# Cross attention: scores by row in six units, and the two halves of dense at other places in TensorE's order

## What is computed

```
cq  = heads(rms_norm(hidden) @ cq_w)                      # 112 tokens, 16 heads
ck, cv = split(encoder_outputs @ ckv_w)                   # 375 rows
p   = softmax(cq * scale @ ck.T)                          # per head, not causal
hidden = hidden + (p @ cv) @ cdense_w                     # "context", then "dense"
```

## Time and profile before

| | us |
|---|---|
| median of 3 runs (2385.53 to 2386.26) | 2385.78 |
| the profiled execution | 2383.2 |
| its span | 2381.4 |
| TensorE busy, share of the span | 2174.7, 91% |
| VectorE busy | 1342.4, 56% |
| ScalarE busy | 1073.9, 45% |
| cross attention, from the first scores to the last copy | 1082 to 1663 |

### The profile page before, as it was taken

The page is one execution under the profiler, slowest core; times in us unless marked ns, Lnnn a source line. Parts: engine busy times, 40 slices in busy tenths (PEclk is TensorE's granted clock), DMA queues, the critical chain, the costliest instruction groups (busy, mean ns, idle before and its releaser), DMA issues.

```text
span 2381.4 us, 46501 instructions
## 1 busy us (share of the span) xinstructions
PE 2174.7 (91%) x19368; PEld 1820.1 (76%) x19368; DVE 1342.4 (56%) x1887; ACT 1073.9 (45%) x1842; POOL 841.8 (35%) x706
## 2 busy tenths in 40 slices
PE   5899996999879988988999999997899999999998
PEld 4899985887756667876777777775788888888887
DVE  4655545877669994435666666663444434435332
ACT  4334434333157774533555555554434434334432
POOL 1101017677513213540222111110555555555553
PEclk8999998999979998997999999999899999999999
DMA  6334335565454445632111111110643443443331
GB/s 201 133 115 141 123 88 180 202 234 208 146 169 130 138 121 215 253 149 74 49 41 41 49 39 49 41 33 29 222 146 124 137 131 120 148 133 109 111 116 45
DMA packets 107057, 293.56 MB, mean 123 GB/s; under 512 B 14424, under 2 KB 18360, under 8 KB 100216
## 3 DMA queue, kind: packets, MB, share of 16 engines
q1 hardware_dynamic: 86624, 229.63, 29.9%
q0 software_dynamic: 18720, 60.29, 6.9%
q10 hardware_dynamic: 1504, 0.68, 0.1%
HBM read 221.36 MB, written 69.18 MB: 122 GB/s over the span
## 4 chain that ended last, share of the span: by engine, by line
PE 73%; DVE 17%; ACT 4%; DMA 3%; issue 2%; POOL 1%; SPq 0%; POOLq 0%; DVEq 0%; ACTq 0%
PE ps L109 19%; PE ps L111 18%; PE ps L110 18%; PE ps L1554 4%; PE ps L1573 3%; PE ps L1591 3%; DVE f_arena L1166 3%; DVE c_max L1161 3%; DVE f_arena L962 3%; ACT f_arena L1474 3%; DVE c_sum L1172 2%; DMA f_arena<-mem_t 1%; PE ps L607 1%; DVE f_arena L958 1%; PE ps L1576 1%
## 5 line engine op out<-in xcount | busy, mean ns | idle before, releaser
L109 PE MATMUL ps<-r_arena 128*128 128x512 f32 (+6 forms) x2410 | 905.6, 376 | 39.1 <-DVE r_arena L177 18.2
L177 POOL TENSOR_TENSOR r_arena<-f_arena,r_arena 128x512 fp32r<-128x512 f32 (+1 forms) x438 | 586.5, 1364 | 868.7 <-ACT r_arena L1455 438.4
L111 PE MATMUL ps<-r_arena 128*128 128x512 f32 (+6 forms) x2410 | 883.8, 367 | 0.0
L110 PE MATMUL ps<-r_arena 128*128 128x512 f32 (+6 forms) x2410 | 883.6, 367 | 0.0
L109 PEld LDWEIGHTS ps<-r_arena 128*128 128x128 f32 (+2 forms) x2410 | 456.0, 189 | 131.8 <-issue 37.6
L111 PEld LDWEIGHTS ps<-r_arena 128*128 128x128 f32 (+2 forms) x2410 | 455.9, 189 | 66.1
L110 PEld LDWEIGHTS ps<-r_arena 128*128 128x128 f32 (+2 forms) x2410 | 457.0, 190 | 60.1
L199 ACT CAST r_arena<-f_arena 128x512 fp32r<-128x512 f32 x400 | 235.5, 620 | 171.3 <-PE ps L111 131.7
L1675 DVE TENSOR_REDUCE e_negmax<-ps 112x3 f32<-112x1125 f32 (+1 forms) x160 | 225.2, 1408 | 106.7 <-PE ps L1554 103.8
L1474 ACT ACTIVATE f_arena<-ps 125x1792 f32<-125x1792 f32 x96 | 159.9, 1666 | 97.9 <-PE ps L1576 97.4
L1959 DVE SCALAR_TENSOR_TENSOR f_arena<-f_arena,ps 128x512 f32<-128x512 f32 (+1 forms) x88 | 57.4, 652 | 234.8 <-ACT f_arena L1850 234.8
(11 more groups left out here) (197 smaller groups left out, 2714.9 us busy)
## 6 DMA issues: line engine op xcount, KB each, us to landing
f_arena<-weights SPq DMA_DIRECT2D x400, 256.0 KB, 3.0
f_arena<-rows SPq DMA_DIRECT2D x14, 1160.0 KB, 5.2
f_arena<-qk_rows SPq DMA_DIRECT2D x32, 448.0 KB, 3.9
f_arena<-mem_e SPq DMA_DIRECT2D x32, 376.0 KB, 3.1
f_arena<-mem_t SPq DMA_DIRECT2D x16, 750.0 KB, 9.8
f_arena<-mem_n SPq DMA_DIRECT2D x8, 1500.0 KB
h_rows<-f_arena SPq DMA_DIRECT2D x7, 1160.0 KB, 4.8
f_arena<-h_rows SPq DMA_DIRECT2D x7, 1160.0 KB, 5.2
```

The costliest lines, as they stand in the source:

```text
L109: first = pe.matmul(out, w_hi, x_hi, start=start, stop=False)
L110: pe.matmul(out, w_hi, x_lo, start=False, stop=False)
L111: return first, pe.matmul(out, w_lo, x_hi, start=False, stop=stop)
L177: return engine.tensor_tensor(out, source, high.bitcast(F32), ALU.subtract)
```

## The change

Scores by row go from five units to six: four of three heads and two of two heads, so that none is in bank 3 any more. Two waits go with that: the last unit's wait for the copy out of bank 3, and context's wait for all maxima. In TensorE's order dense half 0 moves behind scores 3, and dense half 1 behind scores 4, ahead of the new scores 5. The orders of ScalarE, VectorE, GpSimd and SyncE are not changed, but for VectorE's sixth maximum, which its loop over the units brings.

```diff
-S_UNITS, KEY_UNITS = 5, 3
+S_UNITS, KEY_UNITS = 6, 3
@@
-        s_heads = [range(3 * u, 3 * u + 3 if u < S_UNITS - 1 else HEADS) for u in range(S_UNITS)]
+        s_heads = [range(3 * u, 3 * u + 3) for u in range(4)] + [range(12, 14), range(14, 16)]
@@ scores(b, u)
-                if u == S_UNITS - 1 and b >= 2:
-                    pe.wait_ge(e_cd_out, b - 1)
@@ context(b, t)
-                if t == 0:
-                    pe.wait_ge(e_maxed, S_UNITS * min(b + 2, BATCHES))
@@ TensorE's loop
                     scores(s, 2)
                 if 1 <= s <= BATCHES:
                     scores_by_key(s - 1, 0)
-                if s >= 2:
-                    dense(s - 2, 0)
                 if s < BATCHES:
                     scores(s, 3)
                 if s >= 2:
-                    dense(s - 2, 1)
+                    dense(s - 2, 0)
                 if 1 <= s <= BATCHES:
                     scores_by_key(s - 1, 1)
                 if s < BATCHES:
                     scores(s, 4)
+                if s >= 2:
+                    dense(s - 2, 1)
+                if s < BATCHES:
+                    scores(s, 5)
                 if 1 <= s <= BATCHES:
                     scores_by_key(s - 1, 2)
                 if s + 1 < BATCHES:
```

## The result

The changed kernel takes 2480.07 us (median of 4 runs, 2475.86 to 2481.95) against 2386.02 us (4 runs) before: a ratio of 1.0391, 95% interval 1.0373 to 1.0409. It is slower by 94 us. I had forecast 48.7 us more, and a range that ended at 2462 us. The profiled execution took 2481.95 us, its span 2480.1 us.

What follows compares the result with a forecast made beforehand. TensorE, busy 91% of the span, was taken to set the pace, with one hole before key unit 2. Terms 45.3 + 1.6 + 0.4 + 1.4 = 48.7 us on 2385.8 gave 2434.5 us; range 2425 to 2462.

Steps and rivals of the forecast that it cites:

- The chain through ScalarE's queue: Full steps: dense's copy waits for dense half 1, exponentials queue behind it, key unit 2 waits; 1.51 us more a step.
- 30 full steps x 1.51: Cross attention, steps 2 to 31, with both dense and scores: 1.51 us more each, 45.3 us in all.
- Two units for one: Four-head scores unit split into two and two: nothing in full steps, 1.6 us more in the first, 0.4 in the second.
- The 0.4 us for the second step: Second step of the stage, which has no dense: key unit 2 loads 0.4 us later, 0.8 at the lower clock.
- Waits taken out: Scores 4's wait for the copy of dense's result and context's wait for all maxima: removing them changes nothing.
- The end: Step after the last scores: exponential 1 starts at 1652.47 instead of 1651.10, 1.4 us more.
- The clock falls too: Rival: TensorE's clock falls in full steps, up to 2.9 us each; one step in three adds 29 us, 2464 us; chance 0.17.
- The first rival: Full steps: the copy does not delay exponential 1; 0.39 us more a step, 2399.5 us in all; chance 0.09.
- The faster rival: Full steps: exponentials alone set the pace, 0.34 us less a step, some 2377 us in all; chance 0.02.
- the reduction's bound: The two-head maximum takes at least 0.89 us; the faster rival needed under 0.45 us.
- the step's bounds: Extra time of a full step taken as 1.35 to 1.80 us, given as 2428 to 2446 us for the kernel.
- The wait of 1.25 us: Before the change, TensorE's matmuls wait 1.25 us ahead of key unit 2 for exponential 1, 28 times in full steps.

Runs made afterwards that it cites:

- the run with only the small units: The changed kernel with six units kept but both halves of dense back behind key unit 0 and scores 3; 2408.84 us, ratio 1.0084.

## Why the prediction was right in its mechanism and wrong in its sum

- **The chain through ScalarE's queue: right.** Forecast were loads at 2.20, 2.89, 3.77, 4.64, 5.33, 6.47 and 8.53; the trace has 2.21, 2.92, 3.81, 4.68, 5.39, 6.49 and 8.58. The term "30 full steps x 1.51" measures 1.53 in the run with two useless matmuls. The swap of two ScalarE instructions shows the cause. The runs with two and with five useless matmuls behave as the kernel that I forecast, at full clock in all full steps, and took 2433.9 and 2433.7 us for 2434.5. From the first scores to the last copy of the stage the trace with two is 49.3 us longer than before, for 48.7. That is 42.8 in the 28 steps (forecast 42.3), 1.3 ahead of them (2.0), 1.6 in the two steps behind them (3.0) and 3.5 in the end (1.4). That the three small terms make up for each other is luck.
- **The Trainium skill's rule** from "PSUM — Partial Sum Buffer", section "Engine vs sequencer instructions", that ScalarE's queue is strict first in, first out: the trace agrees. Exponential 1 stood ready for 1.9 us (key unit 1 done by about 1361.3, start at 1363.18) behind a copy that waited.
- **Two units for one: right.** The reduction of two heads takes 0.94 us, as forecast, and in full steps it hides behind the exponential. In the first step the loads follow each other by 2.31 and 2.38 us, 4.69 for the forecast 4.78. The 0.4 us for the second step did not come: key unit 2 loads 6.93 us behind scores 2 there, and 6.99 before. Without its cover the sixth unit costs 0.68 us a step, in the run with only the small units.
- **Waits taken out:** nothing in the offsets speaks against the forecast that they cost and give nothing, but they were not tried by themselves, so it is not shown.
- **The end: too small.** Behind the 28 steps the forecast had 3.0 us for two more full steps and 1.4 us for the end. In the changed kernel these are 5.9 us (17.69 and 17.89 us, clock 0.90 and 0.77, for 15.63 and 14.05 us at 0.93 and 0.96) and 5.1 us (19.09 us at 0.68 for 13.96 at 1.00).
- **"The clock falls too": this is the step that failed.** The forecast held the clock at 1.00 and so put the fall at nothing. I gave the rival 0.17 and priced it with one step in three at 2.9 us, 29 us in all. The mechanism was named, and its sign. The frequency was wrong: the clock fell in each full step that was read. The price of one fall was too high: 1.48 us in the changed kernel (3.3 us at 0.50), where I took half of the one long fall in the second step of before. 2.8 us does occur, where the clock stays at 0.50 for 6.7 us. Thirty falls at 1.48 us are 44 us, which with the forecast 48.7 make some 2479 us for the 2480.07 measured.
- What should have moved the chance: by my own working TensorE would be busy 1.9 us of 3.40 ahead of key unit 2 (measured 1.93). Before, 1.66 had come ahead of a fall and 2.17 of none. "Between the two" left it open, and 0.17 was too low for that. The share alone would not have settled it: by the table above it doesn't put the kernels in order. "One step in three" had no row either. The runs have kernels with a fall in every step, in 21, 18 and 2 of 28, and in none. With none and all as bounds, and the price of 2.9 us, the range would have been 2434 to 2521 us.
- The first rival, a copy that holds nothing up, is the kernel with ScalarE's order swapped: 2397.7 us measured for 2399.5.
- The faster rival was excluded by the reduction's bound, and that held.
- Slips in the sum that change nothing: the step's bounds, 1.35 and 1.80 us, give 2430 to 2443 us, not 2428 to 2446, and a step at 1.3 us gives 2428, not 2425. The wait of 1.25 us holds for 20 of the 28 steps of the earlier trace rows; in the eight in which ScalarE casts a weight it is 0.94 to 0.96 us.

What stays open: why the clock fell in each step of the changed kernel but in two of three with half an exponential added, and in every second one for part of the run with only half 0 moved back. The runs show two things. With nothing else changed, a longer wait brings falls, and matmuls put into the wait take them away. They do not show what decides about a single step. The 14.6 us between the spans that lie outside the 28 steps are 3.1 before cross attention begins (its first scores at 1085.25, before at 1082.15) and 12.0 in the first and last steps of the stage; behind the stage the changed kernel is 0.4 faster. For what lies ahead of the stage no run shows a cause in the change. In the ten traces the first scores come between 1082.2 and 1087.6 us, though no edit touches the work ahead of them.

## What to carry to other kernels

When a step is moved on one engine, look at who consumes it on the others, and what stands behind that consumer in its queue: here the consumer was cheap (0.59 us) and did nothing but wait, and the instruction behind it set the pace. Then work out how idle TensorE becomes around the wait. If that is more than the profile shows anywhere in the loop at full clock, carry the fall as a term of the sum with bounds from no step to every step, and not as an unlikely rival. A few useless matmuls in the wait tell the two losses apart in one run.

## What the runs showed that I had not expected

- Two useless 112x512 matmuls in each step, which TensorE streams in about 0.7 us, give back 46 us (2480.1 to 2433.9): the clock stays at 1.00 with TensorE busy 2.57 of 3.40 us around the wait, and goes to 0.50 after 1.93 of 3.40. This is no rule for other orders of work: with half an exponential added it stayed at 1.00 after 1.34 of 3.40 in one step and fell after 1.35 in the next.
- One fall costs 1.45 to 1.48 us where the clock is back after 3.3 us, and 2.8 us where it takes 6.7 us.
- When scores units of two heads stand directly ahead of a key unit, the loads of the key unit mix with those of scores (heads 14 and 15 use two of the four groups of 32 rows, and the other two are free): in the run with only the small units the first load of key unit 2 comes 0.22 us behind the first of scores 5, ahead of the last two of scores, and not 0.57 us behind as after a unit of three.

```profile
1411.44 0.27 PEld L1552 LDWEIGHTS ps<-r_arena 32*112 32x112 f32 x4 [1.36 <-DVE e_negmax L1672]
1411.66 0.18 PEld L1571 LDWEIGHTS ps<-r_arena 32*125 32x125 f32 x2
1411.70 0.18 PEld L1552 LDWEIGHTS ps<-r_arena 32*112 32x112 f32 x2
```
